# Decoder layer: gate logits apart from the shared expert, which moves behind the last chunk

## The reference, cut to what matters

```python
probs = jax.nn.softmax(flat @ gate_W, axis=-1)
topk_w, topk_idx = jax.lax.top_k(probs, TOP_K)           # TOP_K = 2
topk_w = topk_w / topk_w.sum(axis=-1, keepdims=True)
combine = (jax.nn.one_hot(topk_idx, n_exp) * topk_w[..., None]).sum(axis=1)
out = 0.5 * jax.nn.gelu(flat @ shared_W + shared_b, approximate=False)
for e in range(n_exp):
    h = jax.nn.gelu(flat @ W1[e] + b1[e], approximate=False)
    out = out + combine[:, e:e + 1] * (h @ W2[e] + b2[e])
mean, var = out.mean(-1), out.var(-1)
out = (out - mean) * jax.lax.rsqrt(var + LN_EPS) * gamma + beta   # LN_EPS = 1e-5
```

## Time and profile before

| | us |
|---|---|
| median of 3 runs | 889.28 (888.96 to 893.94) |
| the profiled execution | 892.9 |
| its span | 890.8 |

### The profile page before, as it was taken

The page is one execution under the profiler, slowest core; times in us unless marked ns, Lnnn a source line. Parts: engine busy times, 40 slices in busy tenths (PEclk is TensorE's granted clock), DMA queues, the critical chain, the costliest instruction groups (busy, mean ns, idle before and its releaser), DMA issues. The chain is left out here.

```text
span 890.8 us, 17915 instructions
## 1 busy us (share of the span) xinstructions
PE 770.0 (86%) x6633; PEld 438.2 (49%) x6634; DVE 380.3 (43%) x1042; ACT 398.7 (45%) x510; POOL 165.1 (19%) x125
## 2 busy tenths in 40 slices
PE   2997999999999998969799943599999999999830
PEld 1462554645444444324345432367666776667530
DVE  5770412021433434544354564164444444444337
ACT  2657888887988986233233303111111111111113
POOL 5002221000000002020041242931222112221320
PEclk9997999999999999869999966799999999999975
DMA  9698799952362300700030093544444444544443
GB/s 212 187 240 172 210 228 173 312 74 36 41 74 39 37 2 2 296 0 1 10 134 19 31 333 122 179 148 121 97 123 119 118 115 102 124 118 118 79 112 100
DMA packets 78080, 105.96 MB, mean 119 GB/s; under 512 B 9164, under 2 KB 63142, under 8 KB 77860
## 3 DMA queue, kind: packets, MB, share of 16 engines
q1 hardware_dynamic: 70716, 93.53, 41.1%
q0 software_dynamic: 7296, 11.47, 6.9%
HBM read 66.04 MB, written 38.94 MB: 118 GB/s over the span
## 5 line engine op out<-in xcount | busy, mean ns | idle before, releaser
L723 ACT ACTIVATE arena<-ps 128x1024 f32<-128x1024 f32 x256 | 241.5, 1034 | 38.2 <-PE ps L1581 37.5
L1581 PE MATMUL ps<-arena 99*32 99x512 bf16 x2048 | 169.0, 389 | 5.4 <-issue 2.8
L1558 PE MATMUL ps<-arena 128*32 128x256 f32 x2048 | 165.8, 380 | 0.8 <-issue 0.7
L1864 PE MATMUL ps<-arena 128*128 x280 | 129.7, 607 | 0.6 <-ACT arena L801 0.5
L1881 PE MATMUL ps<-arena,xh_tag 128*128 x560 | 126.9, 380 | 2.0 <-DVE xh_tag L1306 1.4
L1881 PEld LDWEIGHTS ps<-arena,xh_tag 128*128 128x128 f32 x560 | 103.7, 190 | 15.6 <-issue 2.9
L801 ACT COPY arena<-ps 128x256 f32<-128x256 f32 x35 | 13.0, 373 | 201.5 <-PE ps L1854 201.5
L647 POOL DMA_INDIRECT sums_by_row<-arena x39 | 60.2, 1545 | 216.1 <-DVE arena L1328 214.9
L1558 PEld LDWEIGHTS ps<-arena 128*32 128x32 f32 x2048 | 69.3, 111 | 53.0 <-issue 4.0
L1301 DVE TENSOR_TENSOR xh_tag<-ps,xh_tag 128x1024 f32<-128x1024 f32 x35 | 42.9, 1224 | 89.4 <-PE ps L1864 89.4
L1864 PEld LDWEIGHTS ps<-arena 128*128 128x128 f32 x280 | 51.7, 195 | 53.7 <-issue 53.7
(11 more groups left out here) (226 smaller groups left out, 810.6 us busy)
## 6 DMA issues: line engine op xcount, KB each, us to landing
xh_tag<-in_L_ffn_b SPq DMA_DIRECT2D x35, 512.0 KB, 3.8
rows_by_expert<-arena SPq DMA_DIRECT2D x9, 1950.0 KB, 18.9
arena<-in_L_ffn_W SPq DMA_DIRECT2D x16, 1024.0 KB, 10.1
arena<-k_parts SPq DMA_DIRECT2D x48, 128.0 KB
arena<-q_parts SPq DMA_DIRECT2D x48, 128.0 KB
arena<-rows_by_expert SPq DMA_DIRECT2D x35, 130.0 KB, 2.1
arena<-in_L_ffn_b SPq DMA_DIRECT2D x35, 128.0 KB, 3.1
q_parts<-arena SPq DMA_DIRECT2D x8, 384.0 KB, 2.6
```

Of the source, the lines that this page charges most:

```text
L723: nc.scalar.activation(probs_of(stage, h), ps[:, 2 * (u % 2):2 * (u % 2) + 2, :].rearrange("p a n -> p (a n)"), ACT.Exp, scale=float(D) ** ...
L1558: last = nc.tensor.matmul(ps[32 * h:32 * h + 32, 4 + half, at:at + 256], v_grp[n % 2][:, kt, h, :], probs_of(stage, h)[:, 256 * part:256 * ...
L1581: last = nc.tensor.matmul(ps[c:c + 32, 2 * (u % 2) + half, :], k_stk[buf][:, h, P * st + c:P * st + c + 32], q_stk[buf][:, h, 512 * half:5 ...
L1864: last = nc.tensor.matmul(ps[:, half, :], xs_t[:, buf, k, :], w1_sb[:, bass.ds(e, 1), k, 512 * half:512 * (half + 1)].squeeze(1), start=(k ...
```

## The change

It does six things.

- PE's `gates(ch)` computes the logits of four tiles, 8 columns each, into one bank; ACT copies all 32 columns at once. It takes the place of `shared_and_gate` in each chunk. The transposed rows x3_t now keep all four chunks, in the memory of acc.
- PE's `shared(ch, p)` computes the shared expert of two tiles: the bias as a product of the identity with the broadcast bias row, and the weights' product added in PSUM. The calls stand behind the last chunk's output product: three ahead of rows3(3), one between gates(3) and ranks(3), four behind the counts. They use banks 0 to 3.
- ACT's `shared_results` takes Gelu straight from PSUM into acc. POOL's four additions of the bias go.
- Expert weights are doubled (1/(0.5 + 0.5 over)), so that the sum is twice what it was; the last epsilon is 4e-5 in place of 1e-5, and POOL's halving goes.
- POOL adds the last bias to x in eight pieces of two tiles, one behind each of the first eight result DMAs.
- SP's load of the last W2 no longer waits for the shared products. A scratch array of DVE moves.

```diff
+        x3_t = acc.rearrange("p t f -> p (t f)").rearrange("p (c k n) -> p c k n", c=NT // CHUNK, k=KC)
...
-            sp.wait_ge(sg_ps, NT)
             sp.wait_ge(slot_ready, NT // CHUNK)
             load_w2(5)
...
-                pool.wait_ge(sg_read, CHUNK * (ch + 1))
-                rows = acc[:, CHUNK * ch:CHUNK * (ch + 1), :]
-                nc.gpsimd.tensor_tensor(rows, rows, shared_b_sb.unsqueeze(1).to_broadcast([P, CHUNK, D]), ALU.add)\
-                    .then_inc(sh_added, 1)
-            pool.wait_ge(sg_act, NT // 4)
-            nc.gpsimd.tensor_scalar(acc, acc, 0.5, None, ALU.mult).then_inc(halved, 1)
-            pool.wait_ge(halved, 1)
+            pool.wait_ge(sg_act, NT // 2)
             pool.dma_start(sums_dram[0:NT * P, :].rearrange("(p t) f -> p t f", t=NT), acc).then_inc(sums_set, 16)
...
-            nc.gpsimd.tensor_tensor(x_sb[:, :, :], x_sb[:, :, :], ffn_b_sb.unsqueeze(1).to_broadcast([P, NT, D]),
-                                    ALU.add).then_inc(x_shifted, 1)
...
                 add_result((n - 1) % 2, n, row_at[:, (n - 1) % 2:(n - 1) % 2 + 1], sums_set)
+                if n <= NT // 2:
+                    rows = x_sb[:, 2 * n - 2:2 * n, :]
+                    last = nc.gpsimd.tensor_tensor(rows, rows, ffn_b_sb.unsqueeze(1).to_broadcast([P, 2, D]), ALU.add)
...
-                for t in range(CHUNK):
-                    act.wait_ge(sg_ps, CHUNK * ch + t + 1)
-                    nc.scalar.copy(logits[:, t, :], ps[:, 6 + t % 2, D:D + EXPERTS]).then_inc(gate_read, 1)
-                    nc.scalar.copy(acc[:, CHUNK * ch + t, :], ps[:, 6 + t % 2, 0:D]).then_inc(sg_read, 1)
+                act.wait_ge(gate_ps, ch + 1)
+                nc.scalar.copy(logits.rearrange("p t e -> p (t e)"), ps[:, 6, 0:CHUNK * EXPERTS]).then_inc(gate_read, 1)
+
+            def shared_results(ch):
+                act.wait_ge(sg_ps, 2 * ch + 2)
+                for p in range(2):
+                    nc.scalar.activation(acc[:, CHUNK * ch + 2 * p:CHUNK * ch + 2 * p + 2, :],
+                                         ps[:, 2 * (ch % 2) + p, :].rearrange("p (t f) -> p t f", t=2), ACT.Gelu).then_inc(sg_act, 1)
...
-                link(nc.vector.tensor_scalar(over_one, over[:, rows], 1.0, None, ALU.add))
+                link(nc.vector.tensor_scalar(over_one, over[:, rows], 0.5, 0.5, ALU.mult, ALU.add))
...
+            def gates(ch):
+
+                if ch == 0:
+                    pe.wait_ge(sgw_in, 32)
+                pe.wait_ge(x3_ready, 2 * (ch + 1))
+                for t in range(CHUNK):
                     for k in range(KC):
-                        last = nc.tensor.matmul(ps[:, 6 + t % 2, 0:D + EXPERTS], x3_t[:, k, P * t:P * (t + 1)],
-                                                sgw_sb[:, k, :], start=(k == 0), stop=(k == KC - 1))
-                    last.then_inc(sg_ps, 1)
+                        last = nc.tensor.matmul(ps[:, 6, EXPERTS * t:EXPERTS * (t + 1)], x3_t[:, ch, k, P * t:P * (t + 1)],
+                                                sgw_sb[:, k, D:D + EXPERTS], start=(k == 0), stop=(k == KC - 1))
+                last.then_inc(gate_ps, 1)
+
+            def shared(ch, p):
+
+                if ch >= 2:
+                    pe.wait_ge(sg_act, 2 * (ch - 1))
+                bank = ps[:, 2 * (ch % 2) + p, :]
+                nc.tensor.matmul(bank, ident[:, :], shared_b_sb.unsqueeze(1).to_broadcast([P, 2, D]), start=True, stop=False)
+                for t in range(2):
+                    for k in range(KC):
+                        last = nc.tensor.matmul(bank[:, D * t:D * (t + 1)], x3_t[:, ch, k, P * (2 * p + t):P * (2 * p + t + 1)],
+                                                sgw_sb[:, k, 0:D], start=False, stop=(t == 1 and k == KC - 1))
+                last.then_inc(sg_ps, 1)
```

64 lines of the change are left out of this document (30 added, 34 removed).

## The result

The changed kernel takes 888.12 us (median of 20 runs, 883.22 to 896.3) beside 893.01 us for the kernel before on the same chip (20 runs, 888.96 to 895.66): a ratio of 0.995, 95% interval 0.9932 to 0.9969. The forecast was 877.4 us. One run of E7 further down (896.25 us) is over 1.5% above the fastest of its kernel and is left out of that kernel's median and interval. The profiled execution took 887.1 us, with a span of 885.0 and a mean granted clock of 0.941 of full.

What follows compares the result with a forecast made beforehand. One chain through all engines in the tail, up to the experts' first rows, was taken as the bound; -7.1 - 1.75 - 0.7 - 3.5 + 2.0 - 0.85 = -11.9 us on 889.28 gave 877.4 us, range 872 to 884.

Steps and rivals of the forecast that it cites:

- part 3: Last chunk: transposes at full clock, -0.7 us, and gates alone with the choice 2.2 us after their first pass, -3.5 us.
- part 5: POOL's 2 MB write of the sums, now beside SP's first row loads, delays the rows: +2.0 us, bounds 0 and +6.3.
- part 1: Gates alone in chunks 0 to 2: shorter passes on PE and one copy bring -7.1 us, 2.3 of it in chunk 1.
- 2 and 3, shared block, transposes, last gates: Tail: shared calls in PE's idle time and no POOL addition, -1.75 us; last transposes, -0.7; last gates, -3.5.
- 3, last sentence: Last chunk: the 2.57 us shared call between gates and ranks ends before DVE's choice, 2.75 us after its start.
- 4, tables: ACT's two more table loads for Gelu and Exp lie in waits or beside DVE's choice and cost 0.
- 6, x's row in pieces: Early expert tiles: adding the bias to x in eight pieces removes a DVE stall at the second tile, -0.85 us.
- the sums write holds the first rows: Rival at the first row loads: they land with the write's end, +6.3 instead of +2.0 us, 881.7 us; chance 0.13.
- DVE did not stall on the pieces: Rival in the expert loop: each x piece holds a DVE operation for 1.11 us, 8.9 us in all, 886.3 us; chance 0.07.
- PE did not run the three calls of the shared block at 1.2 GHz: Rival from output product to first expert tile: PE stays at half clock through the shared block, 892.6 us; chance 0.06.
- The rival that wanted the clock up before the turned outputs: Rival ahead of the last output product: the clock doesn't fall, 3.5 us off, 873.9 us; chance 0.14.
- the signs that the prediction named for being wrong: Gates over 3 us, half clock in the shared block, or first rows landing more than 5 us behind their issue.

Runs made afterwards that it cites:

- E7: The changed kernel with POOL's addition of the bias to x put back into one whole operation; 889.36 us.
- E3: The changed kernel with gate passes of 64 columns instead of 8, the other 56 unread; 883.55 us.
- E5: The changed kernel with the fourth shared-expert call moved behind the last chunk's rank counts; 884.45 us.
- E2: The changed kernel with the write of the sums waiting until the first two expert tiles' rows and b1 rows have landed; 884.75 us.
- E1: The changed kernel again, without any edit; 887.60 us.
- E4: The changed kernel with one shared-expert call moved ahead of the last head group's turned outputs; 887.57 us.
- E9: E8 with E4's early call added; 878.69 us, 0.9840 of the kernel before.
- E6: The changed kernel with eleven unread 512-column products behind the last shared call, in PE's wait for the rows; 883.58 us.
- E8: The changed kernel with E2's late write, E3's wide gate passes and seven unread products; 881.53 us.
- E10: E8 without the unread products, so E2's and E3's edits on the changed kernel; 881.59 us.
- E11: E9 without the unread products, so E2's, E3's and E4's edits on the changed kernel; 880.85 us.
- E12: E9 again, the same code; 879.18 us, 0.9836 of the kernel before.

## Why the prediction was wrong, step by step

The choice of the last chunk came 12.5 us earlier for a forecast of 13.0, so the rearrangement itself was understood. What failed is how much of this reaches the end. Two steps had no price at all: that the call between gates and ranks ends before the choice does (part 3; it cost 1.1 us), and that the experts take over the lead whole (the first tile cost 2.3 us). Two terms were mis-sized: the write of the sums (part 5, +3.4 us for +2.0) and the gates in chunk 1 (part 1, 1.3 us gained for 2.3). Behind three of the four stands the granted clock.

**The base.** The forecast laid -11.9 us on a median of three runs, 889.28. With 20 runs that median is 893.01, so 3.7 of the 10.7 us between forecast and result were there before any argument. The rest is in the sum: 7.0 us in the medians, and 6.1 in the two profiled executions (887.1 us for 881.0), which the parts below account for.

**1, gates alone in the chunks: size missed.** The passes take 1.95 us (forecast 1.97) and the choice starts 2.3 us behind the first (forecast 2.2). In chunk 0 the gain is 2.57 us (2.5 forecast). In chunk 1 it is 1.28 instead of 2.3, because PE fell to 1.2 GHz behind the passes. The term held that a step in which PE is busy costs only its duration; E3 gets back 0.9 of the 1.0 us that it left out. In chunk 2 the gain is 2.2 us in the first profile.

**2 and 3, shared block, transposes, last gates: right.** Three calls at 2.58 us each at a clock of 1.00 (forecast 2.57), and the transposes at once behind them. The three terms -1.75, -0.7 and -3.5 measured -2.0 (from the output product's start to the transposes), -0.9 and -3.4, together -6.3 for -5.95. The 2.94 us operation of DVE is gone. The choice came at 531.04 against 530.5.

**3, last sentence: wrong.** "The call between gates and ranks (2.57 us) ends before the choice does." It took 4.5 us at a falling clock (L1751 at 530.58, L1754 to 535.11), and the ranks waited for it for 1.1 us, shown by E3 and E5 in two ways.

**4, tables: right.** All loads 1.28 us, and the one for Exp runs beside DVE's choice.

**5, write of the sums: mis-sized, +3.4 instead of +2.0.** 2.7 us of it is the landing, and 0.6 is SP's issue, which stands 3.95 us behind the start of the last scatter instead of 3.31; E2 takes both away. The bounds of 0 and +6.3 held. The forecast took from the 9.8 us row that a small load is not kept behind a whole large write. It isn't kept wholly behind it, but it gets no quick turn either: in that row, too, the bias load asked for at 573.88 lands at 583.7, and the write of 573.45 ends at 583.6. The rows landed 0.3 us behind the end of a write that began 2.98 us ahead of them.

**6, x's row in pieces: right number, wrong cause.** The second tile gained 1.23 us (0.85 forecast), but E7 gives the same without the pieces, and the stall had reached PE through SP's load of the fourth tile and not through DVE's copy. That the number came out near is luck.

**What no term had.** The first tile at 1.2 GHz, 2.3 us more than before. The prediction took the time from the rows' landing on as given, "because the 35 expert tiles behind it run at PE's pace whatever stands ahead": they do from the second on, the first does not. And 1.4 us behind the last result product, which is not the change's: 38.2 us before, 39.62 after, but 37.86 in E1 and 38.2 in E2 with the same code there.

**The rivals.** That the sums write holds the first rows, which "land with its end", was the right mechanism at half its price: it cost 3.4 us and not 6.3. The write took 7.5 us here and not 10.1, and the price was too high even by the forecast's own places: 10.1 us, less 2.3 by which the write is ahead of the load, less 2.2 that the rows take alone, is 5.6. DVE did not stall on the pieces (L1313 0.21 us throughout). PE did not run the three calls of the shared block at 1.2 GHz, only the one between gates and ranks. The rival that wanted the clock up before the turned outputs did not come true in the changed kernel; E4 and E9 made it true by filling the wait. Of the signs that the prediction named for being wrong none appeared in the first profile: gates of 1.95 us, the three calls at full clock, rows 4.94 us behind their issue where it had asked for over 5. What the chances, 0.72 for over 1% faster, lacked is this: they had no case in which several small losses come together, and a fall of the clock was thought of only as something that follows from PE's idle time.

## What to carry to other kernels

When an edit turns wide passes into narrow ones, look at the granted clock behind them and not only at their duration: PE can be busy all the time and still be given half its clock, and here widening the passes to 64 columns cost 0.05 us and kept it. A stage that ends earlier uncovers what waited behind it: ask for each transfer that used to come later (here the 2 MB write) what it now lies beside, and for the next stage at which clock PE arrives. Here a small load asked for in the middle of the large write landed at the write's end, wherever the collision was moved to. A saving made at the front should be followed to the last operation in a table of differences, as above, since the place where it disappears is seldom the place that was edited.

## What the hardware showed beyond expectation

- Sixteen 8-column float32 passes, 1.95 us in which PE and its weight loads show no gap, were followed by a fall of the granted clock to 0.50 in chunk 1 and in the last chunk, in the profiles of the changed kernel, E1, E2 and E7 (E4, E5 and E6 show it in chunk 1; in the tail E4's and E5's fall lies beside waits of PE, and E6's follows the passes as in E1). Sixteen 64-column passes were followed by no fall in chunk 1 in any of the six profiles with them, nor at the last choice in E3, E8 and E10; in E9, E11 and E12, where the early call makes PE wait ahead of the gates, the clock fell there in spite of the width. The narrow passes do not always bring the fall: in chunk 0 only one of seven profiles has it (E6), and in chunk 2 E4, where PE has the early call to do behind them, stays at 1.00. The Trainium skill (TensorE: Matmul & The Clock Gate, Part 1, What's actually happening) lets the gate follow how busy PE has been. Rows in which PE is busy for 4.00 of 4.00 us and the clock falls from 1.00 to 0.50 do not agree, if busy is read as the profile prints it.
- After such a fall the same instructions take nearly twice as long: L1754 3.35 us in one place, 1.89 in the next.
- Beside the 2 MB write of the sums a load of 130 KB landed 0.2 to 0.6 us behind the write's end in all eleven profiles in which it was asked for 0.5 us or more behind the write's start (4.4 to 7.9 us behind its issue). It landed in 1.9, 2.0 and 2.4 us in E8, in the kernel before (both 0.67 us ahead of the write) and in E9 (0.12 us behind its start).
- In three kernels (E4, E11, E12) ACT began a copy 1.37 to 1.45 us behind the end of the transposes it waits for; in E9, with the same order, it did not. The traces name no other releaser. This stays open.
- The last tile's result product ran mostly at 1.2 GHz in some executions (5.31 to 5.40 us, 6.55 in E9) and at 2.4 GHz in others (3.71), also of the same code (5.35 in the first profile of the changed kernel, 3.71 in E1; 6.55 in E9, 3.72 in E12): some 1.7 us of the scatter between executions is there.
- Single executions of one kernel differ by up to 13.1 us (the changed kernel, 883.22 to 896.3), and the mean clock goes with them: E4's fastest had 878.88 us at 0.953, its slowest 889.77 at 0.943.
